# A decoder layer with cross attention: VectorE copies out the piece that a bank holds when it changes hands, and the value bias is added in the copy of the values

## The reference

```python
def _L0_xattn_ref(x, c, Wq, bq, Wkv, bkv, q_gamma, k_gamma):
    q = x @ Wq.T + bq
    q = q.reshape(b, n, H, DH).transpose(0, 2, 1, 3)
    kv = c @ Wkv.T + bkv
    kv = kv.reshape(b, m, H, DH, 2).transpose(0, 2, 1, 3, 4)
    k = kv[..., 0]
    v = kv[..., 1]
    q = _rms_norm(q, q_gamma)
    k = _rms_norm(k, k_gamma)
    scores = jnp.einsum('bhnd,bhmd->bhnm', q, k) * scale
    attn = jax.nn.softmax(scores, axis=-1)
    out = jnp.einsum('bhnm,bhmd->bhnd', attn, v)
    return out.transpose(0, 2, 1, 3).reshape(b, n, H * DH)

x = x + _L0_xattn_ref(_layernorm(x, axis=-1), ctx_1024, ...)
```

## Time and profile before

| | before |
|---|---|
| median of 3 runs | 1333.23 us (1331.01 to 1335.4) |
| span of the profiled execution | 1332.3 us |
| TensorE busy | 1201.7 us, 90% |
| ScalarE busy | 905.6 us, 68% |
| GpSimd busy | 704.8 us, 53% |
| VectorE busy | 668.8 us, 50% |
| mean granted clock of TensorE | 0.972 |

### The profile page before, as it was taken

How to read it: one execution, slowest core, us unless ns; L and a number is a source line. 1 busy time by engine, 2 the same in 40 slices (tenths; PEclk the granted TensorE clock), 3 DMA queues, 4 the chain that set the end, 5 groups by cost and what they waited for, 6 DMA issues and landing times.

```text
span 1332.3 us, 27722 instructions
## 1 busy us (share of the span) xinstructions
PE 1201.7 (90%) x8670; PEld 733.6 (55%) x8670; DVE 668.8 (50%) x2202; ACT 905.6 (68%) x1821; POOL 704.8 (53%) x810
## 2 busy tenths in 40 slices
PE   5999999999999896899999999999999989999960
PEld 4666776676677474443334333433322479889950
DVE  6666467557555557555035503552554253333328
ACT  4666456546645615667986798679999749889950
POOL 1776557656656701445415541553367757776640
PEclk9999999999999998899999999999999999999985
DMA  7998665435435721000002000101165476665559
GB/s 236 356 342 273 212 216 192 162 138 200 170 136 185 237 63 34 26 21 23 17 1 56 27 17 2 50 3 33 50 247 181 157 266 200 207 216 180 177 168 379
DMA packets 146755, 195.05 MB, mean 146 GB/s; under 512 B 12048, under 2 KB 132512, under 8 KB 145968
## 3 DMA queue, kind: packets, MB, share of 16 engines
q1 hardware_dynamic: 135856, 162.97, 37.4%
q0 software_dynamic: 10752, 30.26, 6.3%
HBM read 71.01 MB, written 122.18 MB: 145 GB/s over the span
## 4 chain that ended last, share of the span: by engine, by line
PE 63%; ACT 13%; issue 8%; DVE 7%; DMA 4%; POOL 3%; SPq 1%; ACTq 0%; POOLq 0%; DVEq 0%
PE sa_pf L348 11%; ACT xa_probs L1392 8%; PE xa_banks L1231 7%; PE mo_banks L2103 7%; PE xa_banks L1246 6%; PE sa_po L423 5%; PE sa_ps L397 5%; PE xa_banks L1114 5%; PE sa_ptr L408 5%; PE sa_pf L381 4%; PE mo_banks L2112 3%; PE mo_banks L2091 2%; DMA mo_w_all<-in_down_p 1%; DMA mo_w_all<-slots 1%; ACT xa_q_aug L1338 1%
## 5 line engine op out<-in xcount | busy, mean ns | idle before, releaser
L1392 ACT ACTIVATE xa_probs<-xa_banks 128x1024 f32<-128x1024 f32 (+1 forms) x416 | 401.9, 1045 | 83.0 <-PE xa_banks L1231 82.0
L335 POOL TENSOR_SCALAR sa_probs<-sa_probs,sa_recip 128x128 f32<-128x128 f32 (+3 forms) x256 | 275.4, 1090 | 175.9 <-DVE sa_recip L586 175.6
L466 ACT ACTIVATE sa_probs<-sa_probs,sa_neg_max 128x128 f32<-128x128 f32 (+3 forms) x256 | 141.9, 555 | 148.1 <-DVE sa_neg_max L523 148.1
L1246 PE MATMUL xa_banks<-xa_probs,xa_v_one 128*17 128x512 f32 (+1 forms) x1664 | 218.7, 598 | 6.9 <-ACT xa_q_aug L1338 4.6
L1231 PE MATMUL xa_banks<-xa_q_aug,xa_k_aug 32*128 32x512 f32 (+1 forms) x1664 | 153.3, 442 | 13.3 <-issue 3.4
L2019 POOL DMA_INDIRECT slots<-mo_y,mo_dest x128 | 123.0, 961 | 56.4 <-issue 46.4
L2103 PE MATMUL mo_banks<-mo_xs_t,mo_gu 128*128 128x128 f32 x1024 | 136.1, 276 | 0.0
L523 DVE CUSTOM_DVE_ANT_0 sa_probs<-sa_ps,sa_toeplitz 128x128 f32<-128x128 f32 (+3 forms) x256 | 115.5, 488 | 38.7 <-PE sa_ps L397 35.8
L2103 PEld LDWEIGHTS mo_banks<-mo_xs_t,mo_gu 128*128 128x128 f32 x1024 | 125.4, 193 | 0.2
L1231 PEld LDWEIGHTS xa_banks<-xa_q_aug,xa_k_aug 32*128 32x128 f32 (+1 forms) x1664 | 61.5, 179 | 106.3 <-ACT xa_probs L1392 75.5
L583 DVE COPY sa_pt<-sa_ptr 128x128 f32<-128x128 f32 (+3 forms) x128 | 62.8, 490 | 103.8 <-PE sa_ptr L408 103.7
(11 more groups left out here) (321 smaller groups left out, 2269.0 us busy)
## 6 DMA issues: line engine op xcount, KB each, us to landing
rows<-sa_blank SPq DMA_DIRECT2D x128, 548.0 KB, 3.7
mo_xs<-rows SPq DMA_DIRECT2D x128, 137.0 KB
slots<-sa_blank SPq DMA_DIRECT2D x48, 256.0 KB, 6.1
mo_w_all<-slots SPq DMA_DIRECT2D x24, 512.0 KB, 13.2
xa_raw<-in_ctx_t SPq DMA_DIRECT2D x24, 256.0 KB, 2.8
mo_w_all<-in_gate_up_p SPq DMA_DIRECT2D x2, 2816.0 KB, 16.8
sa_toeplitz<-extended_bias SPq DMA_DIRECT2D x8, 512.0 KB, 7.6
mo_w_all<-in_down_p SPq DMA_DIRECT2D x2, 2048.0 KB, 17.1
```

The source lines that it names most:

```text
L335: pool.tensor_scalar(probs[:, t % SLOTS, 0:w], probs[:, t % SLOTS, 0:w], recip[:, col:col + 1], None, ALU.mult).then_inc(probs_ready, 1)
L466: act.activation(probs[:, t % SLOTS, 0:w], probs[:, t % SLOTS, 0:w], ACT.Exp, bias=neg_max[:, i:i + 1], scale=-1.0, accum_out=sums[:, i:i ...
L1246: last = pe.matmul(banks[32 * i:32 * i + XD + 1, 6 + group % 2, :], v_one[b % 2][0:m, c, 4 * g + i, :], probs[0:m, (2 * j + i // 2) % RING ...
L1392: act.activation(probs[0:m, n % RING, :, :], banks[0:m, 2 * (n % 3):2 * (n % 3) + 2, :], ACT.Exp).then_inc(probs_ready, 1)
```

## The change

`by_scalar` now decides who copies a piece. For the piece that a bank holds when it changes hands (slots 14, 27 and 40 of the batches b = 0 to 2; slot 1 was VectorE's already) that is VectorE, so nine copies move from ScalarE to it. The value bias is added on VectorE in the copy of the values, in the 39 `kv` pieces of b = 0 to 2, that is for the values of batches 1 to 3. GpSimd adds it to x for the first batch alone, since the values of that batch are copied by ScalarE in the opening run; for the others its addition of heads waits for the DMA of x itself.

```diff
--- before.py
+++ after.py
@@ -693,6 +693,10 @@
         b, r = divmod(j, SLOTS)
         return b, r // KT, r % KT, rows_of(r % KT)

+    def by_scalar(b, s, kind):
+        before_change = b >= 0 and (s + 1 - LAG_PV) % KT == 0
+        return kind in ("kt", "qt") and not before_change or b < 0 and kind in ("x", "kv")
+
     def slots_of(b):
         return range(O_AT + 1) if b == B else range(SLOTS)

@@ -721,7 +725,7 @@
             bank = PRO_BANKS[f % 8] if b < 0 else 7 - group % 2
             fill_at[b, s], bank_at[f], before[f] = f, bank, holder.get(bank)
             holder[bank] = f
-            if kind in ("kt", "qt") or b < 0 and kind in ("x", "kv"):
+            if by_scalar(b, s, kind):
                 n_act += 1
             else:
                 n_dve += 1
@@ -1060,14 +1064,16 @@
                         g = (b * SLOTS + s) // KT - 1
                         if g == QUADS * B - 1:
                             continue
-                        if g % QUADS == 0:
-                            pool.wait_ge(x_bv_ready, g // QUADS + 1)
+                        if g == 0:
+                            pool.wait_ge(x_bv_ready, 1)
+                        elif g % QUADS == 0:
+                            pool.wait_ge(x_in, 16 * (b + 1))
                         wait_out(pool, fill_at[b, s])
                         cols = x_sb[:, :, (g % QUADS) * 4 * XD:(g % QUADS + 1) * 4 * XD]
                         pool.tensor_tensor(cols, cols, o_norm[:].rearrange("p t j d -> p t (j d)"),
                                            ALU.add).then_inc(x2_part, 1)
-                    if 0 <= b < B and s == STORE_AT:
-                        pool.wait_ge(x_in, 16 * (b + 1))
+                    if b == 0 and s == STORE_AT:
+                        pool.wait_ge(x_in, 16)
                         pool.tensor_tensor(x_sb[:], x_sb[:],
                                            bkv_row[:, D:2 * D].unsqueeze(1).to_broadcast([P, TT, D]),
                                            ALU.add).then_inc(x_bv_ready, 1)
@@ -1314,7 +1320,7 @@

             def evacuate(b, s):
                 step = step_of(b, s)
-                if step is None or not (step[0] in ("kt", "qt") or b < 0 and step[0] in ("x", "kv")):
+                if step is None or not by_scalar(b, s, step[0]):
                     return
                 kind, i = step[0:2]
                 nb, f = b + 1, fill_at[b, s]
@@ -1536,7 +1542,7 @@

             def evacuate(b, s):
                 step = step_of(b, s)
-                if step is None or step[0] in ("kt", "qt") or b < 0 and step[0] == "x":
+                if step is None or by_scalar(b, s, step[0]) and step[0] != "kv":
                     return
                 kind, i = step[0:2]
                 nb, f = b + 1, fill_at[b, s]
@@ -1564,9 +1570,10 @@
                                       bkv_row[0:m, 0:D], ALU.add).then_inc(k_out, 1)
                     if nb == 0:
                         return
-                    dve.tensor_copy(v_one[nb % 2][0:m, i, :, 0:XD],
-                                    banks[0:m, bank, D:2 * D].rearrange("p (h d) -> p h d", h=H)
-                                    ).then_inc(prep_out, 1)
+                    dve.tensor_tensor(v_one[nb % 2][0:m, i, :, 0:XD],
+                                      banks[0:m, bank, D:2 * D].rearrange("p (h d) -> p h d", h=H),
+                                      bkv_row[0:m, D:2 * D].rearrange("p (h d) -> p h d", h=H), ALU.add
+                                      ).then_inc(prep_out, 1)
                     return
                 dve.wait_ge(prep_psum, f + 1)
                 if kind == "kt":
```

## The result

| | before | after |
|---|---|---|
| median | 1333.38 us (6 runs, 1331.01 to 1335.4) | 1338.66 us (6 runs, 1337.6 to 1341.58) |
| span of the profiled execution | 1332.3 us | 1338.5 us |
| TensorE, ScalarE busy | 1201.7, 905.6 us | 1205.4, 901.8 us |
| VectorE, GpSimd busy | 668.8, 704.8 us | 675.3, 695.0 us |
| mean granted clock | 0.972 | 0.969 |

The ratio is 1.0042, 95% interval 1.0031 to 1.0052: slower by 5.3 us. The forecast was 1335.9, slower by 2.7, with a range up to 1340.0.

What follows compares the result with a forecast made beforehand. TensorE's own queue was taken to set the time, its waits being what could change. Sum: 2.94 − 1.11 − 0.90 + 0.98 − 0.25 + 1.00 = +2.7 us, or 1335.9; range 1329.5 to 1340.0 us.

Steps and rivals of the forecast that it cites:

- The copy itself: Each 128x512 copy from PSUM: 692 ns on VectorE, 0.65 us on ScalarE; engine change alone worth 0.04 us.
- Slot 14: Three batches: new copy stands behind VectorE's query norm chain, preparing piece follows one product later; +0.98 us each, +2.94.
- Slot 27: Three batches: VectorE is free and copies earlier than ScalarE, so TensorE restarts earlier; −0.37 us each, −1.11.
- Slot 40: First two batches: idle VectorE copies earlier, −0.45 us each, −0.90; third batch: copy waits behind a layernorm, +0.98.
- The value bias: Additions in VectorE's value copies count 0; GpSimd's removed additions and waits give −0.25 us, in the second batch alone.
- GpSimd's collision at slot 7: Second and third batch: GpSimd's context splitting stretches VectorE's L1429 to 1.33 us, as in the first batch; +1.00 us.
- The last batch: Batch 4: GpSimd, rid of addition and wait, sends routed rows earlier; taken as 0, bound −1.0 us.
- The signs: Profile after: kt1 copy ends query chain, batches 133.8, 133.9, 135.6 us; wrong if TensorE waits on VectorE at slots 28, 41.
- rival 1: Slot loop: losses are hidden in TensorE's small waits on ScalarE's exponentials; 1333.2 us, chance 0.12.
- rival 2: ScalarE's queue paces the loop, so nine copies and the waits come off, −10.5 us; 1322.7 us, chance 0.07.
- rival 3: GpSimd's wait for the DMA of x was on the path, 28.4 us would go; 1304.8 us, chance 0.03.
- rival 4: VectorE is late at all nine hand-overs, not four; +9.6 us, 1343 us, chance 0.11.

Runs made afterwards that it cites:

- the two reorderings alone: Kernel before, with only parts two and three of first key group's norm a slot later and query norm's last third behind copies: 1331.06 us, ratio 0.9987.

## Why the prediction was right in its parts and short in its size

- **The copy itself** costs 0.69 us on VectorE (0.68 to 0.69 in all nine places), as the row of L1578 said; the bound with 0.35 us more was never reached. By the rule of the Trainium skill (VectorE: DVE Perf Modes, the section on the TRN2 errata) the swap should have cost 0.09 us each time; the gains at slot 28 came out 0.07 larger than forecast, not smaller. ScalarE's copies of this shape took from 0.60 to 0.79 us in the kernel before, so the 0.09 is there against the shortest of them, but the place in the queue outweighed it.
- **Slot 14, the term that was mis-sized.** "The preparing piece follows one product later" was right in order and in delay: without a fall the step is 0.89 to 0.93 us, against the 0.98 forecast. But the product's duration was taken from a stretch at full clock. The two short waits became one of 2.04 us, the clock fell behind it, and each fall added 1.1 to 1.4 us (2.00 to 2.31 less 0.9). Three falls make 3.9 us; with 0.2 us less for the delays that is the missing 3.65. The prediction foresaw the stretch itself: it has the product 1.83 us later, behind a wait of 0.33, and "about 2 us more idle" among its signs (1.6 to 1.7 measured). But it read the granted clock as 0.99 to 1.00 and did not ask what a single, longer idle stretch does to it. That the lower clock is the 3.9 us is shown by the slots 15 with the same stretch and no fall: 0.9 in one of three with the copies alone, in three of three and in two of three with the key norm moved. That the long stretch brings the fall on is shown by counts only: 12 of 18 with it, none of 21 with the short ones.
- **Slot 27**: −1.34 against −1.11. TensorE restarted 0.15 us after VectorE's copy, where I had put the 0.25 us of a bank copy's release.
- **Slot 40**: −1.21 against −0.90, for the same reason, and +0.88 against +0.98 in the third batch. Here the same risk of the clock was missed: it fell in one of nine profiles.
- **The value bias**: −0.25, as worked out from the two distances; the additions stayed at 0.41 to 0.42 us.
- **GpSimd's collision at slot 7**: +1.05 against +1.00, and the run that moves the norm shows that it is the stretched step ahead of the copy of x1.
- **The last batch**: −0.80 against 0, within its bound of −1.0 but for another reason. Not the sends came earlier to any use; GpSimd's addition of heads no longer ran while VectorE picked experts.
- **The signs.** The order on VectorE and its times held to 0.1 us. The batches, from slot 2 to slot 2, went from 133.3, 133.5 and 133.4 us to 134.6, 134.8 and 136.7, so by 1.3, 1.3 and 3.3 instead of 0.2, 0.4 and 2.1. One sign of being wrong came true and means nothing: TensorE does wait on VectorE at slots 28 and 41 of the first two batches, for 0.28 and 0.21 us. The forecast's own sum had left 0.35 us of wait there, so the sign contradicted it.
- **The rivals.** The losses were not hidden (rival 1): each late copy cost 0.9 us even at full clock. ScalarE does not pace the loop (rival 2): with its nine copies gone nothing came beyond the waits. GpSimd's stall was not on the path (rival 3): without it the bias part is worth nothing, although the chain of waits ran through it. VectorE was late at four hand-overs, not at nine (rival 4).

Without the clock the terms as measured add up to 1.05 − 0.25 + 2.7 − 1.34 − 0.33 − 0.8 = +1.0 us, and the kernel with the scores twice, at +1.0 in its trace, is that case. The forecast of +2.7 was thus 1.7 too high in what it did price and left out 3.9 that it did not; that it came as near as 2.6 us to the measured +5.3 is in part luck.

## What to carry to other kernels

Before a copy moves to an idle engine, look at that engine's queue in the very slot: VectorE was half idle on average, and behind a norm chain it took up the piece 1.9 us late. When two short waits of TensorE merge into one long one, price the work behind it at the lower clock too, and look at several executions, since the fall may come in some of them only. A chain that has slack belongs behind the copies that TensorE waits for: the two reorderings alone brought 2.7 us in the trace, where the change as it stood lost 5.0 and its useful copies were worth 2.55.

## What the hardware showed that was not expected

- Idle stretches of 2.04 us between stretches of dense work dropped the granted clock in nine of nine cases in the changed kernel (2.4 to 1.2 GHz level, 0.57 over the 4 us behind two of them), in two of three with the copies alone, in none of three and one of three in two profiles of one and the same program. The stretch of 1.93 to 1.95 us at slot 41 of the third batch was followed by a fall in one of the nine profiles that show it. Behind 1.57 to 1.59 us there was none in three, behind 1.45 to 1.47 none in six.
- An instruction stream with eight more matmuls in each of three places ran shorter than the one without them: 1.0 us over the kernel before instead of 5.0 in its one trace, and 1336.2 us instead of 1338.3 to 1338.7 in the median.
- VectorE's additions of a PSUM and an SBUF operand kept their 0.42 us beside a working GpSimd, while a step on two SBUF operands went from 0.23 to 1.33 us, and two large ones from 1.16 to 1.39 and 1.57 us beside GpSimd's addition of heads and the send behind it.
